# Attention and routed experts on one core: the last batch's end reordered, weight splits shared with GpSimd, rows without a token given addresses of their own

## The chip, the cores and the metric

The kernel runs on one core of one Trainium2 chip. The metric is the device time of one execution in microseconds (us), less is better; "the span" is the time from the first to the last instruction in the profiled execution. Engines: TensorE (PE in the rows, its weight loads PEld), VectorE (DVE), ScalarE (ACT), GpSimd (POOL) and SyncE (SP), which here only issues transfers. A "q" behind an engine's name is its sequencer, which issues transfers.

## The reference

`x` is 8 batches of 1024 tokens with 256 features, in f32.

```python
x = _layernorm(x + attention(x))           # 16 heads, latent 32, rotary, causal
# mixture of experts: E = 8, top K = 2, DIM = 256, H = 512
gates = softmax(xf @ gate_w); topw, topi = top_k(gates, 2)
topw = topw / sum(topw)
combine = sum(topw * one_hot(topi, 8))
h = gelu(ln(xf @ w1[e] + b1[e]) * ln1_g + ln1_b)   # for every expert e
y = h @ w2[e] + b2[e]
out = ln(sum(y * combine) + xf) * ln_g + ln_b
x = _layernorm(x + out)
```

## The kernel before

The program is a row of blocks; all engines meet at the end of each. In order:

1. `weight_phase`: the attention weights are combined. Here also the DRAM table `token_of_row` (67,584 rows of two integers: which token to read, which row of `y_rows` to write) is filled with "no token": read token 0, write row 2 * B * T, one row past the results. The fill is made by two memsets on VectorE into `no_token` and a transfer on SyncE's queue (line 88).
2. `attention_phase`, main block: 32 units (8 batches by 4 groups of 4 heads). Every engine walks one list of items in the order of `PLACES`, a table of places written out by hand. Items that belong to a batch's end are: `C` (TensorE multiplies the attention output by the projection, VectorE adds it to `z` and takes mean and variance, three instructions), `NORM` (GpSimd: 1/sqrt of the variance by a power), `NX` (VectorE normalizes), `ZT` (TensorE transposes, ScalarE copies to `z_T`), `G` (gate product, VectorE copies 8 logits), `STORE`, `R` (22 small VectorE steps of routing), `CNT` (counts on TensorE), `SCAT` (16 indirect transfers on GpSimd, line 805, which write token numbers into `token_of_row`). Items that use PSUM take turns in a ring of four banks.
3. The last batch's end is a block of its own (lines 864 to 947), because the expert weights take the place of the attention buffers. In it the 16 weight parts (`w1` and `w2` of 8 experts, 128x1024 each) are loaded by ScalarE's queue, and each is split in two: ScalarE makes the rounded high part (line 600), and a subtraction makes the low part in place (line 753, on VectorE); the text calls this subtraction a split. VectorE begins with a memset of the bias buffer, waits for five small tables, then makes splits 0 and 1, all `C` items, splits 2 to 5 between the `NX` items, `G`, `R`, the tables of tiles (lines 914 to 934), and then splits 6 to 15.
4. `expert_phase`: 136 tiles of 128 rows, sorted by expert. Per tile GpSimd gathers rows of `x1` (line 1007), makes a 1/sqrt (line 1013) and scatters the result to `y_rows` (line 1020); TensorE makes both products, each in three passes of high and low parts. ScalarE copies a tile's result out (line 1110). About 1,024 rows of these tiles hold no token. Each result scatter waits first for the landing of the one before it (lines 1018 and 1019).
5. `combine_phase`: 16 groups of 4 tiles are mixed, normalized and stored.

Of the kernel before, what the change touches and what calls it, by code (L numbers as in the profile page):

```python
# [6 lines left out]
F32, F32R, BF16 = mybir.dt.float32, mybir.dt.float32r, mybir.dt.bfloat16  # L7
# [5 lines left out]
P = 128  # L13
# [25 lines left out]
def weight_phase(nc, dram, wts, consts, lat_dram, token_of_row, xs):  # L39


    with ExitStack() as ctx:
# [27 lines left out]
        no_token = sb("no_token", [P, ROWS // P, 2], I32)  # L70
        zero_set = sem("zero_set")
# [8 lines left out]
        def _(sp):  # L80
# [6 lines left out]
            sp.wait_ge(zero_set, 2)  # L87
            sp.dma_start(token_of_row.rearrange("(p s) o -> p s o", p=P), no_token[:]).then_inc(tables_loaded, 16)
# [50 lines left out]
        def _(dve):  # L139
            nc.vector.memset(no_token[:, :, 0], 0).then_inc(zero_set, 1)  # L140
            nc.vector.memset(no_token[:, :, 1], 2 * B * T).then_inc(zero_set, 1)
# [51 lines left out]
def attention_phase(nc, dram, wts, consts, xs, lat_dram, inv_dram, x1_dram, token_of_row, routes, tail, attention,  # L193
# [9 lines left out]
    with ExitStack() as ctx:  # L203
# [66 lines left out]
        def unit_items(n):  # L270
# [36 lines left out]
            if g == GROUPS - 1:  # L307
                for name in ("C", "NX", "ZT", "G"):
                    put(name, *[(name, b, tb) for tb in range(TB)])
                put("NORM", ("NORM", b))  # L310
# [343 lines left out]
        def vector_items(dve, items):  # L654
            for it in items:
# [93 lines left out]
                elif kind == "W":  # L749
                    dve.wait_ge(w_hi_ready, n + 1)  # L750
# [22 lines left out]
        def gpsimd_items(pool, items, zero):  # L773
            for it in items:
# [21 lines left out]
                elif kind == "NORM":  # L796
# [3 lines left out]
                    nc.gpsimd.tensor_tensor(z_rstd[:], z_ve[:], half[:], ALU.pow).then_inc(rstd_ready, 1)  # L800
                elif kind == "SCAT":
# [7 lines left out]
        with nc.Block() as block:  # L809
# [20 lines left out]
            def _(pool):  # L830
# [21 lines left out]
        w_hi_ready, w_lo_ready = sem("e_hi_ready"), sem("e_lo_ready")  # L852
# [5 lines left out]
        scat_at, c_at = [it[0] for it in late].index("SCAT"), [it[0] for it in late].index("C")  # L858
        between = [x for it in late[c_at:scat_at] for x in
                   ((it, ("W", 2 + it[2] // 2)) if it[0] == "NX" and it[2] % 2 else (it,))]  # L860
        late = [("W", 0), ("W", 1)] + late[:c_at] + between + late[scat_at:]
        late_weights = [("W", w) for w in range(6, len(parts))]

        with nc.Block() as block:
# [22 lines left out]
            def _(act):  # L887
                for i, (w, e) in enumerate(parts):
                    act.dma_start(experts[w + "_lo"][:, e, :].bitcast(F32), dram[w][:, e, :]).then_inc(w_loaded[i], 16)
                scalar_items(act, late)  # L890
                scalar_items(act, late_weights)
# [4 lines left out]
            def _(dve):  # L896
                nc.vector.memset(experts["b2"][:].bitcast(F32), 0.0).then_inc(b_zeroed, 1)
                dve.wait_ge(end_tables, 16 * len(table_loads))
# [5 lines left out]
                vector_items(dve, late)  # L904
# [30 lines left out]
                vector_items(dve, late_weights)  # L935
# [559 lines left out]
```

## Time and profile before

| | us |
|---|---|
| runs of the kernel before | 2384.43, 2387.57, 2387.07 (median 2387.07) |
| profiled execution | 2383.96 |
| its span | 2382.2 |
| TensorE busy (share of the span) | 2119.7 (89%) |
| VectorE busy | 1715.5 (72%) |
| ScalarE busy | 1366.8 (57%) |
| GpSimd busy | 1296.8 (54%) |
| mean granted TensorE clock | 0.922 of full |

The profiled execution is one run; 1.8 us lie around its span. Busy shares are averages over blocks with different limits, so each block has to be read by itself: times below are counted from the span's start. A row of a timeline holds start, duration, engine, line and operation, how many instructions it merges (x5), and in brackets how long the engine stood idle before it and what released it. "issue" as a releaser is time in which the profile shows no wait.

### The profile page before, as it was taken

To read this page: it belongs to the slowest core of one execution; us is meant where nothing else is said; L and a number is where in the kernel's file an instruction comes from. 1 tells how busy PE (TensorE), PEld (TensorE's weight loads), DVE (VectorE), ACT (ScalarE), POOL (GpSimd) and SP (SyncE) were. 2 spreads that over 40 slices of the span, in tenths; PEclk is the share of its full clock that TensorE was granted. 3 is DMA by queue.
4 is the path that set the end of the run, shared out by engine and by line. 5 is a ranking of instruction groups with operands and counts; after the bars stand their busy time and mean duration, and the time that the engine had idled before them with its cause. 6 is when DMAs were issued, how large, how long until landed. Compare 5 with 4: busy or idle time off the path is not lost. (4 is left out here: it accounts for less than half of the span.)

```text
span 2382.2 us, 43666 instructions
## 1 busy us (share of the span) xinstructions
PE 2119.7 (89%) x12268; PEld 1476.8 (62%) x12268; DVE 1715.5 (72%) x5003; ACT 1366.8 (57%) x3316; POOL 1296.8 (54%) x1472
## 2 busy tenths in 40 slices
PE   3898998999899999899899989974399999999598
PEld 2654655565555556465566555533299989988487
DVE  3675687687577677668668767815588888888498
ACT  1265655555555565565565555653278778778254
POOL 2455465655754763666556475551677777776000
PEclk7798999999899898899899899985699999999799
DMA  6555556556555555554655555615022222222575
GB/s 181 123 137 129 113 114 160 116 113 156 116 118 147 121 122 123 133 121 108 163 111 126 143 119 115 135 24 199 23 75 75 75 73 75 75 73 66 165 245 169
DMA packets 190519, 284.47 MB, mean 119 GB/s; under 512 B 54072, under 2 KB 111056, under 8 KB 190160
## 3 DMA queue, kind: packets, MB, share of 16 engines
q1 hardware_dynamic: 168720, 236.43, 41.7%
q0 software_dynamic: 17152, 35.81, 5.0%
q10 hardware_dynamic: 4416, 9.44, 1.1%
q8 instruction: 110, 1.80, 0.3%
q14 instruction: 121, 0.99, 0.2%
HBM read 99.48 MB, written 37.90 MB: 58 GB/s over the span
## 5 line engine op out<-in xcount | busy, mean ns | idle before, releaser
L546 ACT ACTIVATE probs<-scores_T 128x512 f32<-128x512 f32 (+3 forms) x1536 | 654.7, 492 | 256.4 <-PE scores_T L435 253.0
L785 POOL TENSOR_SCALAR_AFFINE_SELECT probs<-probs 128x256 f32<-128x256 f32 x512 | 205.7, 410 | 540.1 <-ACT probs L546 537.4
L494 PE MATMUL ring<-k_stack,q_stack_b 96*128 96x512 f32 (+3 forms) x1024 | 400.7, 434 | 19.9 <-DVE neg_part L693 9.5
L693 DVE TENSOR_REDUCE neg_part<-ring 128x1 f32<-128x512 f32 x512 | 333.5, 684 | 97.5 <-PE ring L494 95.4
L435 PE MATMUL scores_T<-q_stack_b,k_stack 98*128 98x512 f32 (+3 forms) x1024 | 325.9, 396 | 43.8 <-ACT probs L546 42.7
L452 PE MATMUL o_ps<-probs,v_ones 128*17 128x512 f32 (+3 forms) x3072 | 349.6, 529 | 1.4 <-POOL probs L785 1.1
L494 PEld LDWEIGHTS ring<-k_stack,q_stack_b 96*128 96x128 f32 x1024 | 195.4, 200 | 228.4 <-issue 75.1
L698 DVE CUSTOM_DVE_ANT_0 ring<-ring,mask 128x384 f32<-128x384 f32 (+3 forms) x512 | 243.6, 507 | 120.4 <-PE ring L494 118.1
L698 DVE CUSTOM_DVE_ANT_0 ring<-ring,mask,neg_part 128x384 f32<-128x384 f32 (+3 forms) x512 | 260.5, 554 | 74.2 <-PE ring L494 73.4
L1099 ACT ACTIVATE o_sb<-ht_ps,ln_b,ln_g 128x128 f32<-128x128 f32 x544 | 217.9, 450 | 89.4 <-PE ht_ps L1048 89.0
L435 PEld LDWEIGHTS scores_T<-q_stack_b,k_stack 98*128 98x128 f32 x1024 | 192.0, 204 | 101.5 <-ACT probs L546 78.2
L554 ACT ACTIVATE u<-ring,lat_bias 128x512 f32<-128x512 f32 x128 | 88.0, 689 | 195.9 <-PE ring L476 184.3
L476 PE MATMUL ring<-x_hi,lat_w 128*128 128x512 f32 x512 | 189.8, 413 | 8.4 <-DMA lat_w<-lat_split 8.4
L494 PE MATMUL ring<-k_stack,q_stack_a 96*128 96x384 f32 (+3 forms) x512 | 171.8, 369 | 27.4 <-DMA k_stack<-u_rot 22.7
L762 POOL TENSOR_TENSOR u<-u,cos 128x512 f32<-128x512 f32 x126 | 162.1, 1287 | 36.6 <-DMA u_rot<-u 36.3
L1020 POOL DMA_INDIRECT y_rows<-z,tok x136 | 145.0, 1066 | 56.6 <-issue 33.7
L1007 POOL DMA_INDIRECT z<-x,tok x136 | 142.2, 1046 | 48.0 <-issue 40.0
L805 POOL DMA_INDIRECT token_of_row<-ids,slot x128 | 141.4, 1104 | 49.0 <-DVE ids_f L652 25.9
L770 POOL TENSOR_TENSOR u<-u,u_rot 128x512 f32<-128x512 f32 x126 | 162.4, 1289 | 9.2
L1060 PE MATMUL y_ps<-w_hi,g_hi 128*128 x544 | 165.1, 303 | 2.4 <-DVE g_lo L1126 1.7
L765 POOL TENSOR_TENSOR u_rot<-u_rot,sin 128x512 f32<-128x512 f32 x126 | 163.7, 1300 | 0.1
L494 PEld LDWEIGHTS ring<-k_stack,q_stack_a 96*128 96x128 f32 x512 | 93.6, 195 | 98.3 <-DVE neg_max L698 51.0
(191 smaller groups left out, 4617.1 us busy)
## 6 DMA issues: line engine op xcount, KB each, us to landing
u_rot<-u SPq DMA_DIRECT2D x128, 256.0 KB, 3.8
k_stack<-u_rot SPq DMA_DIRECT2D x128, 256.0 KB, 4.2
lat_w<-lat_split SPq DMA_DIRECT2D x32, 512.0 KB, 5.9
q_stack_a<-u_rot SPq DMA_DIRECT2D x64, 256.0 KB
q_stack_b<-u_rot SPq DMA_DIRECT2D x64, 256.0 KB
k_stack<-u SPq DMA_DIRECT2D x64, 256.0 KB, 4.3
y<-y_rows SPq DMA_DIRECT2D x32, 512.0 KB, 6.4
x_raw<-in_xT SPq DMA_DIRECT2D x16, 512.0 KB, 6.1
```

What stands on the lines that cost most here:

```text
L435: nc.tensor.matmul(sc[(t + j) % 3][:, HALF - w:HALF], k_stack[:, n % 2, h, P * kb:P * kb + P], q_stack[c][:, row_buf(n, c), h, q0 - HALF * ...
L452: last = nc.tensor.matmul(o_ps[32 * h:32 * h + VW, q0 - HALF * c:HALF], v_ones[:, b % 2, kb, HG * g + h, :], probs[:, s % 2, h, cols], sta ...
L476: last = nc.tensor.matmul(out[:], lat_w[:, kc, side, w_, :], a[:, kc, cols], start=i == 0, stop=i == 5)
L494: nc.tensor.matmul(out[:, 0:k1 - k0], q_stack[qb // 4][0:3 * L, row_buf(n, qb // 4), h, P * (qb % 4):P * (qb % 4) + P], k_stack[0:3 * L, n ...
L546: nc.scalar.activation(probs[:, s % 2, h, cols], sc[(t + j) % 3][:, HALF - w:HALF], ACT.Exp).then_inc(exp_done, 1)
L693: nc.vector.tensor_reduce(neg_part[:, n % 2, part_col], src[:], AX_X, ALU.max, negate=True).then_inc(max_taken, 1)
L698: nc.vector.tensor_tensor_reduce(out=src[:, 0:w], in0=src[:, 0:w], in1=consts["mask"][:, HALF - w:HALF], scale=-1.0, scalar=neg_part[:, n ...
L765: ops.tensor_tensor(u_rot[s][:, cols], u_rot[s][:, cols], consts["sin"][:, cols], ALU.mult).then_inc(sin_done[s], 1)
L770: ops.tensor_tensor(u[s][:, cols], u[s][:, cols], u_rot[s][:, cols], ALU.add).then_inc(rope_done[s], 1)
L785: nc.gpsimd.affine_select(both, both, [[0, 2], [1, P]], ALU.is_ge, zero, base=0, channel_multiplier=-1).then_inc(kept, 1)
L1060: nc.tensor.matmul(y_ps[j % 2][:, 0:C], a[j % 2][:, f, :], experts[w][:, bass.ds(e, 1), C * f:C * f + C], start=f == 0 and a is g_hi and w ...
L1099: nc.scalar.activation(g[k % 2][:, f, :], ht_ps[k % 2][:, P * f:P * f + P], ACT.Gelu, bias=experts["ln1_b"][:, f, bass.ds(e, 1)], scale=ex ...
```

## The change

Four edits.

- The table of empty rows comes from a kernel input `no_token` in DRAM, and row r of `token_of_row` without a token now writes row 2 * B * T + r of `y_rows`, which has grown by as many rows. The memsets and the wait for them are gone.
- A tile's result scatter no longer waits for the landing of the one before.
- In the last batch the transposes `ZT` stand one place earlier, so that the next tile's transpose comes ahead of this tile's gate product on TensorE. VectorE takes the `C` items ahead of the table wait.
- Splits 10 to 15 are made by GpSimd: 10, 11, 12 ahead of `NORM`, 13, 14, 15 between `NORM` and the scatters. VectorE makes splits 0 and 1 ahead of the first `G` and one behind each `G`. Weights are loaded and rounded in the order of `hi_order`: eight high parts ahead of the first `ZT` copy, one behind each.

```diff
-        no_token = sb("no_token", [P, ROWS // P, 2], I32)
-            sp.wait_ge(zero_set, 2)
-            sp.dma_start(token_of_row.rearrange("(p s) o -> p s o", p=P), no_token[:]).then_inc(tables_loaded, 16)
+            sp.dma_start(token_of_row.rearrange("(p s) o -> p s o", p=P), dram["no_token"]).then_inc(tables_loaded, 16)
-            nc.vector.memset(no_token[:, :, 0], 0).then_inc(zero_set, 1)
-            nc.vector.memset(no_token[:, :, 1], 2 * B * T).then_inc(zero_set, 1)
...
-                for name in ("C", "NX", "ZT", "G"):
+                for name in ("C", "NX", "G"):
                     put(name, *[(name, b, tb) for tb in range(TB)])
+                first, pace = PLACES["ZT"]
+                ahead = 1 if b == B - 1 else 0
+                at += [(first - ahead + pace * tb, ("ZT", b, tb)) for tb in range(TB)]
...
                 elif kind == "W":
-                    dve.wait_ge(w_hi_ready, n + 1)
+                    dve.wait_ge(w_hi_ready, hi_order.index(n) + 1)
...
+                elif kind == "W":
+                    pool.wait_ge(w_hi_ready, hi_order.index(n) + 1)
+                    w, e = parts[n]
+                    lo = experts[w + "_lo"][:, e, :]
+                    nc.gpsimd.tensor_tensor(lo, lo.bitcast(F32), experts[w + "_hi"][:, e, :].bitcast(F32),
+                                            ALU.subtract).then_inc(w_lo2_ready, 1)
...
-        scat_at, c_at = [it[0] for it in late].index("SCAT"), [it[0] for it in late].index("C")
-        between = [x for it in late[c_at:scat_at] for x in
-                   ((it, ("W", 2 + it[2] // 2)) if it[0] == "NX" and it[2] % 2 else (it,))]
-        late = [("W", 0), ("W", 1)] + late[:c_at] + between + late[scat_at:]
-        late_weights = [("W", w) for w in range(6, len(parts))]
+        weights = lambda a, b: [("W", w) for w in range(a, b)]
+        zt_at, c_end = late.index(("ZT", B - 1, 0)), late.index(("C", B - 1, TB - 1)) + 1
+        hi_order = (10, 0, 11, 1, 12, 2, 3, 13, 14, 4, 15, 5, 6, 7, 8, 9)
+        g_at = late.index(("G", B - 1, 0))
+        late_act = late[:zt_at] + [("W", w) for w in hi_order[:TB]] + [
+            x for it in late[zt_at:] for x in ((it, ("W", hi_order[TB + it[2]])) if it[0] == "ZT" else (it,))]
+        late_dve = late[c_end:g_at] + weights(0, 2) + [
+            x for it in late[g_at:] for x in ((it, ("W", 2 + it[2])) if it[0] == "G" else (it,))]
+        norm_at, scat_at = late.index(("NORM", B - 1)), late.index(("SCAT", B - 1, 0, 0))
+        late_pool = (late[:norm_at] + weights(10, 13) + late[norm_at:scat_at] + weights(13, len(parts)) + late[scat_at:])
...
             def _(dve):
                 nc.vector.memset(experts["b2"][:].bitcast(F32), 0.0).then_inc(b_zeroed, 1)
+                vector_items(dve, late[:c_end])
                 dve.wait_ge(end_tables, 16 * len(table_loads))
...
-                vector_items(dve, late)
+                vector_items(dve, late_dve)
...
-                vector_items(dve, late_weights)
                 dve.wait_ge(diff_exp, 1)
...
                     pool.wait_ge(y_ready, j + 1)
-                    if j:
-                        pool.wait_ge(y_stored[(j - 1) % 4], 16 * ((j - 1) // 4 + 1))
                     nc.gpsimd.indirect_dma_start(y_rows, bass.IndirectOffsetOnAxis(tok[:, j % 16, 1:2], 0),
...
-    y_rows = nc.dram_tensor("y_rows", (2 * B * T + 1, C), F32).ap()
+    y_rows = nc.dram_tensor("y_rows", (2 * B * T + ROWS, C), F32).ap()
+        "no_token": np.stack([np.zeros(ROWS), 2 * B * T + np.arange(ROWS)], 1).astype(np.int32).reshape(P, ROWS // P, 2),
```

## Rows read from the trace of the kernel before

**Rows 1.** Windows: length, busy us of PE, PEld, DVE, ACT, POOL; granted clock; DMA.

```profile
1609.00:1660.00 51.00, 24.39 (x89) 18.56 (x89) 25.80 (x74) 16.86 (x23) 4.58 (x4) 0.60 0.63 233
...
1800.00:1900.00 100.00, 100.00 (x697) 91.51 (x696) 86.98 (x221) 80.27 (x222) 78.04 (x85) 1.00 0.26 76
```

**Rows 2.** Timeline of ScalarE, last batch's end.

```profile
1609.38 10.06 ACTq L889 DMA_DIRECT2D w_lo<-in_w  x16
1619.48 4.84 ACT L600 ACTIVATE w_hi<-w_lo 128x1024 fp32r<-128x1024 f32 x5 [21.70 <-issue]
```

**Rows 3.** Timeline of VectorE, last batch's end.

```profile
1620.65 0.23 DVE L899 CAST ones<-rows 128x128 fp32r<-128x128 f32 x1 [9.02 <-DMA rows<-in_rows]
...
1623.72 0.41 DVE L717 TENSOR_TENSOR z<-ring,z 128x256 f32<-128x256 f32 x1
...
1631.52 0.18 DVE L721 BATCH_NORM_AGGREGATE z_mv<-z_stats 128x2 f32<-128x6 f32 x1
1633.84 0.73 DVE L726 TENSOR_SCALAR z<-z,z_mv,z_rstd 128x256 f32<-128x256 f32 x2 [2.13 <-POOL z_rstd L800]
1634.49 1.22 DVE L753 TENSOR_TENSOR w_lo<-w_lo,w_hi 128x1024 fp32r<-128x1024 f32 x1
...
1653.18 0.17 DVE L733 COPY logits<-ring 128x8 f32<-128x8 f32 x1 [1.91 <-PE ring L519]
...
1669.09 11.42 DVE L753 TENSOR_TENSOR w_lo<-w_lo,w_hi 128x1024 fp32r<-128x1024 f32 x10
```

**Rows 4.** Timeline of TensorE, last batch's end.

```profile
1611.95 6.31 PE L505 MATMUL ring<-cproj_w,y_T 128*128 128x256 f32 x16 [14.83 <-POOL y_T L791]
...
1643.83 0.99 PE L519 MATMUL ring<-gate_w,z_T 128*128 128x8 f32 x4 [0.57 <-ACT z_T L596]
```

**Rows 5.** Timeline of GpSimd, last batch's end.

```profile
1631.80 0.25 POOL L798 TENSOR_SCALAR z_ve<-z_mv 128x8 f32<-128x8 f32 x1 [19.99 <-DVE z_mv L721]
1632.13 1.67 POOL L800 TENSOR_TENSOR z_rstd<-z_ve,a_minus_half 128x8 f32<-128x8 f32 x1
1659.69 1.61 POOL L805 DMA_INDIRECT token_of_row<-ids,slot  x1 [25.89 <-DVE ids_f L652]
...
1669.10 12.28 POOL L805 DMA_INDIRECT token_of_row<-ids,slot  x1 [0.30 <-issue]
...
1691.78 0.96 POOL L805 DMA_INDIRECT token_of_row<-ids,slot  x1 [0.30 <-issue]
```

**Rows 6.** Line 791, all instructions: duration in ns, min/median/max.

```profile
L791 POOL TENSOR_TENSOR y_T<-y_T,inv_rep x16: 2346/2378/2822, 220.1 to 1609.5; 128x1024 f32<-128x1024 f32 x16
```

**Rows 7.** Line 684, all instructions, in the same form.

```profile
L684 DVE TENSOR_TENSOR u<-u,u_rot x64: 678/689/2785, 54.6 to 1521.5; 128x512 fp32r<-128x512 f32 x64
```

**Rows 8.** Timeline of VectorE near 415 us.

```profile
415.34 2.43 DVE L684 TENSOR_TENSOR u<-u,u_rot 128x512 fp32r<-128x512 f32 x1 [4.82 <-ACT u_rot L565]
```

**Rows 9.** Timeline of GpSimd near 415 us.

```profile
414.87 2.36 POOL L791 TENSOR_TENSOR y_T<-y_T,inv_rep 128x1024 f32<-128x1024 f32 x1 [0.22 <-DMA inv_rep<-inv_sums]
417.19 1.72 POOL L765 TENSOR_TENSOR u_rot<-u_rot,sin 128x512 f32<-128x512 f32 x1
```

**Rows 10.** Timeline of GpSimd, end of the expert block.

```profile
2199.37 1.30 POOL L1020 DMA_INDIRECT y_rows<-z,tok  x1 [0.20 <-issue]
2202.86 1.02 POOL L1020 DMA_INDIRECT y_rows<-z,tok  x1 [2.19 <-DMA y_rows<-z,tok]
...
2213.62 0.96 POOL L1020 DMA_INDIRECT y_rows<-z,tok  x1 [2.90 <-DMA y_rows<-z,tok]
```

**Rows 11.** Timeline of ScalarE, end of the expert block.

```profile
2205.61 0.38 ACT L1110 ACTIVATE z<-y_ps 128x256 f32<-128x256 f32 x1 [1.59 <-PE y_ps L1063]
```

**Rows 12.** Line 1020 in the window of its last scatter: issue to landing.

```profile
DMA to landing us min/median/max: 3.1/3.1/3.1
```

**Rows 13.** Line 1020, all 136 scatters.

```profile
DMA to landing us min/median/max: 2.5/2.5/4.2
```

**Rows 14.** DMA issues of the start: KB, us from issue to landing.

```profile
token_of_row<-no_token SPq DMA_DIRECT2D x1, 528.0 KB, 8.1
```

More of the change, by code:

```diff
@@ L69, in weight_phase @@
         vo_b_ready, lat_kept = sem("vo_b_ready"), sem("lat_kept")
-        no_token = sb("no_token", [P, ROWS // P, 2], I32)
-        zero_set = sem("zero_set")
         block = ctx.enter_context(nc.Block())
@@ L851, in attention_phase @@
         w_loaded = [sem(f"w_loaded{i}") for i in range(len(parts))]
-        w_hi_ready, w_lo_ready = sem("e_hi_ready"), sem("e_lo_ready")
+        w_hi_ready, w_lo_ready, w_lo2_ready = sem("e_hi_ready"), sem("e_lo_ready"), sem("e_lo2_ready")
         end_tables, b_loaded, ln1_loaded = sem("end_tables"), sem("b_loaded"), sem("ln1_loaded")
@@ L887, in _ @@
             def _(act):
-                for i, (w, e) in enumerate(parts):
+                for i in hi_order:
+                    w, e = parts[i]
                     act.dma_start(experts[w + "_lo"][:, e, :].bitcast(F32), dram[w][:, e, :]).then_inc(w_loaded[i], 16)
-                scalar_items(act, late)
-                scalar_items(act, late_weights)
+                scalar_items(act, late_act)
                 act.wait_ge(routed, R_STEPS * B)
@@ L940, in _ @@
                                         ALU.mult).then_inc(done, 1)
-                dve.wait_ge(w_lo_ready, len(parts))
+                dve.wait_ge(w_lo_ready, 10)
                 dve.wait_ge(done, 1)
@@ L945, in _ @@
             def _(pool):
-                gpsimd_items(pool, late, None)
+                gpsimd_items(pool, late_pool, None)
+                pool.wait_ge(w_lo2_ready, len(parts) - 10)
                 pool.wait_ge(scattered, 16 * 2 * TILES)
```

## Prediction

> **What bounds the kernel now.** I read the windows by stage first, then the timelines of the single engines between 1609 and 1700 us, then what each scatter waits for. The program is a row of blocks, and the change touches three: the weights at the start, the end of the last batch (1609.4 to 1696.6 us), and the expert tiles (1697 to 2222 us). In the expert block TensorE is busy 100.00 us of 100 at full granted clock [rows 1], so what another engine saves there is worth nothing until the last tiles. In the last batch's block TensorE works 24.39 us of 51 [rows 1], and the order is set by a chain across engines. Its stages before: ScalarE issues sixteen weight loads until 1619.4 and makes its first high part then [rows 2]; VectorE waits for a small table until 1620.65, makes two weight splits, and starts the first C item at 1623.72, though TensorE had begun them at 1611.95 [rows 3, 4]; the last variance is there at 1631.70 [rows 3]; GpSimd makes the inverse root by 1633.80 [rows 5]; VectorE normalizes, with four splits between, from 1633.84; the last gate logits come at 1653.35 and routing starts right behind them [rows 3]; then sixteen scatters run on GpSimd from 1659.69 to 1692.73 [rows 5]. One of these took 12.28 us where the last took 0.95, and it began at 1669.10, when VectorE began ten weight splits in a row (1669.09 to 1680.51) [rows 3, 5].
>
> **The change, part by part.** A split is an instruction on VectorE: 11.42 us for ten, 1.14 each [rows 3].
>
> C items. VectorE now takes them before the table wait. TensorE made the first four in 6.31 us [rows 4]; eight at that rate, begun at 1611.95, end at 1624.6. VectorE needs 1.0 us an item (1623.72 to 1631.70 for eight [rows 3]) and follows, so the variances are ready at 1625.6, 6.1 us earlier.
>
> Three splits on GpSimd (weights 10, 11, 12) now stand ahead of the root. The trace has no split on GpSimd. The nearest row is its product over the same 128x1024 elements: 2.35 us shortest, 2.38 median, 2.82 longest of 16 [rows 6]. I take 2.35, for its neighbours here are quiet, and keep 2.82 above; below, nothing suggests less. ScalarE's first high part ends at 1620.5 and each next one 0.95 later [rows 2]; the third one that GpSimd needs is the fifth, at 1624.3, so GpSimd is never short: 1620.5 + 3 x 2.35 = 1627.6. The root takes the 2.0 us from 1631.80 to 1633.80 [rows 5], so it ends at 1629.6 instead of 1633.8: 4.2 us gained, where without the three splits it would have been 6.1. The table casts, moved behind the C items, lie under this wait and cost nothing; uncovered they would be the 0.8 us from 1620.65 to the first split.
>
> What both engines read from SBUF. At 415.34 a VectorE subtraction of two SBUF tensors, 0.69 us at the median [rows 7], took 2.43 [rows 8]: it ended 0.5 us after GpSimd's product, 2.36 us long, ended at 417.23. GpSimd's next product in turn took 1.72 [rows 9], where half of a 2.35 us product is 1.2. The two are not run side by side: who comes second waits for the whole instruction. The Trainium skill says the same in "SBUF — State Buffer", section "Who interferes with whom": an exclusive lock, not a shared bandwidth; this trace agrees. So I let every GpSimd split after the root stand on VectorE's path. Split 13 has its high part (the eighth, 1627.2) and follows the root at once; it meets the first normalization: + 2.35, to 1632.0. Splits 14 and 15 meet VectorE's splits: + 4.7.
>
> Normalizing: eight, 0.65 us a pair (1633.84 to 1634.49) [rows 3], so 2.6, to 1634.6. Then ten splits, 11.4; eight logit copies of at most 0.17 [rows 3], mostly overlapped, 1.0; and the 4.7: routing starts at 1634.6 + 17.1 = 1651.7, 1.7 us earlier. Does TensorE keep up? Before, an iteration was 2.08 us (1.91 idle and 0.17 on VectorE [rows 3]), of which TensorE stood idle 0.57 ahead of the gate product [rows 4]; with the next transpose moved ahead of it this gap fills, and 8 x 1.5 = 12 us from 1632.4 ends at 1644.4, six us before VectorE. ScalarE needs a copy of 0.38 and a high part of 0.95, which also fits. The 8 x 0.57 = 4.6 us that the reordering frees on TensorE are thus worth nothing by themselves: VectorE is later.
>
> Routing to the first scatter is as before, 6.3 us: 1658.0. The scatters took 33.04 us. None of VectorE's splits is left beside them, so the long one becomes 0.96: 33.04 - 11.32 = 21.7. What the routing tables cost them stays (the first took 1.61 [rows 5]). End at 1679.7 instead of 1692.73: **13.0 us**. Bounds of this part: 7.05 more if GpSimd's last three splits run beside VectorE's work; 2.8 less if each of the six takes 2.82.
>
> Expert block. GpSimd loses one wait: a scatter had to wait until the scatter of the tile before had landed. Queued behind it on GpSimd are gathers and roots, for tiles far ahead; TensorE is full, so nothing in the steady part: 0. At the end it counts. The last five scatters started 3.5 to 3.9 us apart (2199.37, 2202.86, ..., 2213.62 [rows 10]), the last though its tile had been copied at 2205.99 [rows 11]. Without the wait: 1.0 us each plus 0.3 issue after 2200.67 gives 2201.0 and 2202.3; the next two wait for ScalarE alone, and the last starts at 2206.1. **7.5 us** gained. The last tiles hold rows without a token, all written to one address; the landing of the last took 3.1 us [rows 12] against a median of 2.5 for all [rows 13]. With rows of their own that is 0 to 0.6 more: I take 0.3.
>
> Start. Two memsets leave VectorE, which idled there until 10.9 us: 0. The table of empty rows comes from DRAM instead of SBUF: same place in SP's queue, same 528 KB, 8.1 us to landing before [rows 14], issued near 10.9, ended near 19.6 with the block ending at 26.2. No row shows a copy from DRAM to DRAM; below nothing, above I let its transfer double, 8 us more, which would end at 27.7 and cost 1.5, or up to 8 if what is queued behind moves with it whole. Bytes and queue stay, so I take 0.
>
> Sum: 13.0 + 7.5 + 0.3 = 20.8. The profiled execution took 2383.96 us (span 2382.2 and 1.8 around it), so its like would be 2363.2. It lay 3.1 below the median of the runs shown, 2387.07, and the same sum on that gives 2366.3; I forecast **2366**.
>
> **Rivals.** (a) *No lock between splits* (12%): GpSimd's last three run beside VectorE's, and 7.05 come on top: 2359. For it: the one long subtraction in [rows 8] could have had another cause. Against: its end, half a us behind GpSimd's.
>
> (b) *The long scatter stays* (8%). If it is not VectorE's splits that held it, but something in the scatter's own queue, 11.3 are not saved: 2378. Against: its start and end fit the ten splits within 0.9 us. The Trainium skill's "SBUF — State Buffer", same section, speaks against my reading: it infers that a two-input `tensor_tensor` takes only the read side and does not stall a GpSimd DMA's descriptors. By the rows it does, or a read of the offsets does; by that rule, this rival.
>
> (c) *Scatters land in turn anyway* (7%), or a second outstanding one waits in the queue: the 7.5 stay lost: 2374. Against: in the code the gaps are the semaphore wait that goes, and GpSimd stood idle 2.90 us ahead of the last one [rows 10].
>
> (d) *GpSimd's splits are dear* (6%), the other side. All six lie on the chain, three ahead of the root and three against VectorE. Each us more per split costs 6. At 2.35 + 20.8/6 = 5.8 us each the gain is gone; at 6.8 the result is 2393. Against: the same engine makes 1024 products in 2.35. A rounding output on GpSimd has no row.
>
> (e) *The copy at the start* (5%) moves the first block by up to 8: 2374.
>
> The rest, 62%, is my forecast, 2362 to 2370 by itself.
>
> **How the numbers follow.** The range leaves out (b) and (d), 14%, and takes in (a), (c), (e): 2357 to 2377. A measurement of this kernel tells about 0.2%, 4.8 us. Slower by more needs the dear half of (d) and what I have overlooked: 5%. No difference needs two rivals at once or the middle of (d): 4%. Faster: 91%.
>
> **What the profile would show.** First C item on VectorE near 1613.6; splits on GpSimd of about 2.4 us, with the root's end at 1629.6; a VectorE normalization or split of about 2.7 or 3.5 us beside each of the last three; routing near 1652; sixteen scatters in 22 us with none over about 2; expert tiles still 3.6 us apart; last four expert scatters 1.3 to 2.1 us apart, the last at ScalarE's last copy. Wrong would be: GpSimd splits of over 3.5 us, a long scatter with no split beside it, or a first block that ends after 26.7.

## The result and the profile after

| | median us | runs | lowest to highest |
|---|---|---|---|
| before | 2387.32 | 4 | 2384.43 to 2389.46 |
| changed | 2353.16 | 4 | 2338.54 to 2364.46 |

The ratio is 0.9862, 95% interval 0.982 to 0.9904: 34 us less, where 20.8 were forecast, and 4 us below the forecast's range. The profiled execution of the changed kernel is its fastest, 2338.54 us (span 2336.8, mean granted clock 0.939; before 2382.2 at 0.922). That difference in clock is the first thing to clear away. The ratios in this document leave out runs over 1.5% above the fastest of their kernel and are not the quotient of the two medians beside them (for p2_wait below the medians would give 0.992, its ratio is 0.9964).

The windows by stage, once for each kernel. The stages are cut at the same issues in both: the first `lat_w` load, the load of `b_raw` (start of the last batch's block), the first `tok` load (start of the expert tiles), the load of `ln_g_rep` (start of the combine stage). Columns as in [rows 1]. The changed kernel:

```profile
27.00:1589.20 1562.20, 1423.70 (x8079) 864.44 (x8079) 1101.78 (x3223) 875.14 (x1977) 887.45 (x1041) 0.94 0.55 125
1589.20:1663.10 73.90, 20.71 (x89) 17.12 (x89) 50.15 (x99) 18.13 (x25) 38.70 (x25) 0.57 0.43 161
1663.10:2177.15 514.05, 495.80 (x3400) 449.86 (x3400) 427.54 (x1088) 395.04 (x1089) 382.51 (x408) 0.98 0.25 72
2177.15:2336.80 159.65, 140.41 (x640) 122.98 (x640) 130.29 (x562) 77.19 (x225) 0.00 (x0) 0.94 0.68 213
```

The kernel before:

```profile
26.20:1609.40 1583.20, 1445.87 (x8079) 875.18 (x8079) 1094.57 (x3223) 876.02 (x1977) 887.56 (x1041) 0.92 0.54 123
1609.40:1697.60 88.20, 24.39 (x89) 18.56 (x89) 46.76 (x105) 18.46 (x25) 32.75 (x19) 0.56 0.37 135
1697.60:2222.20 524.60, 497.91 (x3400) 450.37 (x3400) 431.32 (x1088) 395.10 (x1089) 376.27 (x408) 0.97 0.24 70
2222.20:2382.20 160.00, 140.58 (x640) 123.09 (x640) 130.22 (x562) 77.23 (x225) 0.00 (x0) 0.94 0.68 212
```

The main block, 1583 us long, is the same code in both, with the same 8079 matmuls; TensorE needs 22.2 us less for them at a granted clock of 0.94 than at 0.92, and the block is 21.0 us shorter. Of the 45.4 us between the two spans, only 14.3 (last batch's block), 10.6 (expert tiles) and 0.4 (combine), less 0.8 at the start, lie in stages that the change can touch: 24.5 us. (Over all profiles of the two kernels, two and three, these stages differ by 26.5.) A second profile of the changed kernel (run t_after below), in a run at a mean clock of 0.928, gives the main block the length that it had before:

```profile
26.30:1609.30 1583.00, 1445.66 (x8079) 876.88 (x8079) 1100.98 (x3223) 876.01 (x1977) 888.49 (x1041) 0.92 0.54 123
```

Now the last batch's block. VectorE, in the view of [rows 3]:

```profile
1593.96 0.42 DVE L715 TENSOR_TENSOR z<-ring,z 128x256 f32<-128x256 f32 x1 [2.41 <-PE ring L503]
...
1602.51 0.18 DVE L719 BATCH_NORM_AGGREGATE z_mv<-z_stats 128x2 f32<-128x6 f32 x1
1602.61 0.52 DVE L909 CAST ones<-rows 128x128 fp32r<-128x128 f32 x1
1603.05 2.45 DVE L911 CAST b_hi<-b_raw 8x256 fp32r<-8x256 f32 x1
1605.53 2.46 DVE L913 TENSOR_TENSOR b_lo<-b_raw,b_hi 8x256 fp32r<-8x256 f32 x1
1609.89 4.70 DVE L724 TENSOR_SCALAR z<-z,z_mv,z_rstd 128x256 f32<-128x256 f32 x8 [1.90 <-POOL z_rstd L798]
1614.51 2.35 DVE L751 TENSOR_TENSOR w_lo<-w_lo,w_hi 128x1024 fp32r<-128x1024 f32 x2
...
1616.85 3.30 DVE L751 TENSOR_TENSOR w_lo<-w_lo,w_hi 128x1024 fp32r<-128x1024 f32 x1
...
1620.15 3.29 DVE L751 TENSOR_TENSOR w_lo<-w_lo,w_hi 128x1024 fp32r<-128x1024 f32 x1
...
1623.44 1.21 DVE L751 TENSOR_TENSOR w_lo<-w_lo,w_hi 128x1024 fp32r<-128x1024 f32 x1
...
1630.62 0.21 DVE L609 TENSOR_REDUCE top<-logits 128x8 f32<-128x64 f32 x1
```

GpSimd, in the view of [rows 5]:

```profile
1600.68 7.03 POOL L803 TENSOR_TENSOR w_lo<-w_lo,w_hi 128x1024 fp32r<-128x1024 f32 x3 [8.95 <-ACT w_hi L598]
...
1608.19 1.67 POOL L798 TENSOR_TENSOR z_rstd<-z_ve,a_minus_half 128x8 f32<-128x8 f32 x1
1609.84 2.33 POOL L803 TENSOR_TENSOR w_lo<-w_lo,w_hi 128x1024 fp32r<-128x1024 f32 x1
1614.58 7.78 POOL L803 TENSOR_TENSOR w_lo<-w_lo,w_hi 128x1024 fp32r<-128x1024 f32 x2 [2.40 <-ACT w_hi L598]
1636.77 1.61 POOL L809 DMA_INDIRECT token_of_row<-ids,slot  x1 [14.41 <-DVE ids_f L650]
...
1639.96 2.02 POOL L809 DMA_INDIRECT token_of_row<-ids,slot  x1 [0.30 <-issue]
...
1657.55 0.95 POOL L809 DMA_INDIRECT token_of_row<-ids,slot  x1 [0.30 <-issue]
```

TensorE, in the view of [rows 4], the eight C items:

```profile
1591.88 8.96 PE L503 MATMUL ring<-cproj_w,y_T 128*128 128x256 f32 x32 [14.83 <-POOL y_T L789]
```

In microseconds from the start of the block (1609.4 before, 1589.2 after):

| | before | forecast | after |
|---|---|---|---|
| last variance there | 22.3 | 16.2 | 13.5 |
| inverse root ends | 24.4 | 20.2 | 20.7 |
| eight normalizations end | between splits | 25.2 | 25.4 |
| routing starts | 44.0 | 42.3 | 41.4 |
| first of the sixteen scatters | 50.3 | 48.6 | 47.6 |
| last of them ends | 83.3 | 70.3 | 69.3 |
| block ends | 88.2 | | 73.9 |

A small cast and a small subtraction (8x256 elements) took 2.45 and 2.46 us: they stood behind the GpSimd splits that began at 1600.68. GpSimd's last two splits lost time too: they took 7.78 us together, where one alone takes 2.33. The scatters took 21.73 us (1636.77 to 1658.50); none was over 2.02.

The end of the expert tiles. GpSimd, in the view of [rows 10]:

```profile
2162.55 1.30 POOL L1028 DMA_INDIRECT y_rows<-z,tok  x1 [0.20 <-issue]
2164.15 0.96 POOL L1028 DMA_INDIRECT y_rows<-z,tok  x1 [0.30 <-issue]
2165.41 0.96 POOL L1028 DMA_INDIRECT y_rows<-z,tok  x1 [0.30 <-issue]
2167.47 0.96 POOL L1028 DMA_INDIRECT y_rows<-z,tok  x1 [1.09 <-ACT z L1118]
2169.30 0.96 POOL L1028 DMA_INDIRECT y_rows<-z,tok  x1 [0.88 <-ACT z L1118]
```

ScalarE's last copy, in the view of [rows 11]; then line 1028 in the window of its last two scatters, as [rows 12]; then the copy at the start, as [rows 14]:

```profile
2168.64 0.38 ACT L1118 ACTIVATE z<-y_ps 128x256 f32<-128x256 f32 x1 [1.45 <-PE y_ps L1071]
```

```profile
DMA to landing us min/median/max: 2.4/2.5/2.5
```

```profile
token_of_row<-in_no_token SPq DMA_DIRECT2D x1, 528.0 KB, 7.0
```

From ScalarE's last copy (its end) to the end of the stage it was 2222.2 − 2205.99 = 16.2 us and is 2177.15 − 2169.02 = 8.1. But the stage is 10.6 shorter, not 8.1: the last copy itself comes 2.5 us earlier in it (505.5 us after its start, 508.0 before). The forecast had 0 there.

### The profile page after: what moved, and what is told of

It reads as the page before. It is cut to its first block and busy times, and to the rows that moved or that the text cites. A ratio compares the mean times of both kernels' runs of the same rounds, so it can differ in the third digit from the quotient of the medians.

```text
span 2336.8 us, 43530 instructions
## 1 busy us (share of the span) xinstructions
PE 2092.7 (90%) x12268; PEld 1464.7 (63%) x12268; DVE 1721.4 (74%) x4995; ACT 1365.5 (58%) x3316; POOL 1308.8 (56%) x1478
## 5 line engine op out<-in xcount | busy, mean ns | idle before, releaser
L492 PE MATMUL ring<-k_stack,q_stack_b 96*128 96x512 f32 (+3 forms) x1024 | 396.3, 429 | 22.1 <-DVE neg_part L691 10.4
L433 PE MATMUL scores_T<-q_stack_b,k_stack 98*128 98x512 f32 (+3 forms) x1024 | 318.1, 387 | 45.4 <-ACT probs L544 44.5
L450 PE MATMUL o_ps<-probs,v_ones 128*17 128x512 f32 (+3 forms) x3072 | 341.8, 518 | 2.1 <-POOL probs L783 1.8
L433 PEld LDWEIGHTS scores_T<-q_stack_b,k_stack 98*128 98x128 f32 x1024 | 186.3, 198 | 99.6 <-ACT probs L544 78.6
L492 PE MATMUL ring<-k_stack,q_stack_a 96*128 96x384 f32 (+3 forms) x512 | 170.9, 367 | 25.5 <-DMA k_stack<-u_rot 20.8
L1017 POOL DMA_INDIRECT z<-x,tok x136 | 147.5, 1084 | 47.8 <-issue 40.4
L1068 PE MATMUL y_ps<-w_hi,g_lo 128*128 x544 | 154.2, 283 | 0.0
L1068 PE MATMUL y_ps<-w_lo,g_hi 128*128 x544 | 153.8, 283 | 0.0
```

Of the source, the lines that this page charges most:

```text
L433: nc.tensor.matmul(sc[(t + j) % 3][:, HALF - w:HALF], k_stack[:, n % 2, h, P * kb:P * kb + P], q_stack[c][:, row_buf(n, c), h, q0 - HALF * ...
L450: last = nc.tensor.matmul(o_ps[32 * h:32 * h + VW, q0 - HALF * c:HALF], v_ones[:, b % 2, kb, HG * g + h, :], probs[:, s % 2, h, cols], sta ...
L492: nc.tensor.matmul(out[:, 0:k1 - k0], q_stack[qb // 4][0:3 * L, row_buf(n, qb // 4), h, P * (qb % 4):P * (qb % 4) + P], k_stack[0:3 * L, n ...
L1068: nc.tensor.matmul(y_ps[j % 2][:, 0:C], a[j % 2][:, f, :], experts[w][:, bass.ds(e, 1), C * f:C * f + C], start=f == 0 and a is g_hi and w ...
```

## The experiments

Twelve more entries ran in three groups, repeats among them, each group beside the kernel before on one chip. In each group the kernel before ran 17 to 35 times, and that gave the first surprise: 2362.73 to 2414.33 us, 2357.32 to 2400.63 and 2373.97 to 2401.81, where the three runs shown ahead of the forecast lay within 3.2 us.

**One part alone: s1_start and s2_late.** The first has only the start edit; the second is the changed kernel with the start and the dropped wait undone.

```diff
# s1_start, against the kernel before
-            sp.wait_ge(zero_set, 2)
-            sp.dma_start(token_of_row.rearrange("(p s) o -> p s o", p=P), no_token[:]).then_inc(tables_loaded, 16)
+            sp.dma_start(token_of_row.rearrange("(p s) o -> p s o", p=P), dram["no_token"]).then_inc(tables_loaded, 16)
-            nc.vector.memset(no_token[:, :, 0], 0).then_inc(zero_set, 1)
-            nc.vector.memset(no_token[:, :, 1], 2 * B * T).then_inc(zero_set, 1)
-    y_rows = nc.dram_tensor("y_rows", (2 * B * T + 1, C), F32).ap()
+    y_rows = nc.dram_tensor("y_rows", (2 * B * T + ROWS, C), F32).ap()
# s2_late, against the changed kernel: the lines above turned round, and
+                    if j:
+                        pool.wait_ge(y_stored[(j - 1) % 4], 16 * ((j - 1) // 4 + 1))
```

> The kernel before with the first edit alone: the table of empty rows comes from DRAM, rows without a token have addresses of their own; the scatter's wait and the last batch's end are as before. After the change the main attention block took 20.9 us less in the profiled run although its code is the same, and the first block ended 0.85 us later. Theory S (this edit moves the start of the main block, and that alone changes which stretches of it get the lower granted clock): the main block gets about 10 to 20 us shorter, ratio 0.992 to 0.996. Theory N (this edit does nothing; the main block varies by itself from run to run in every kernel): 0.85 us longer, ratio 1.000 within the spread. My prediction's sum: within 1 us of before.

> The kernel before with the last batch's end alone: reordered, six splits on GpSimd; the start and the scatter's wait are as before. Theory S: the main block is as before (about 1583 us in the profile), the last batch's block 14.4 us shorter, ratio 0.994. Theory C (what comes later in the program, its size or its placement, changes the main block): the main block some 10 us shorter as well, ratio 0.990.

**The start of the main block moved: s3_later3 and s4_later6.** Three or six more additions of 128x256 on VectorE ahead of the last weight of the first block; their result is not used.

```diff
# s3_later3, against the kernel before; s4_later6 has 6
+            for i in range(3):
+                nc.vector.tensor_tensor(pause[:, i, :], m_ps[:, 0:C], cproj_b[:], ALU.add)
             nc.vector.tensor_tensor(wts["z_bias"][:], m_ps[:, 0:C], cproj_b[:], ALU.add).then_inc(split, 1)
```

> The kernel before with three more VectorE additions of 0.3 to 0.4 us (into a buffer that nobody reads) at the end of the first block, so that the main block starts about 1.0 us later. No part of the change is in it. Theory S (start of the main block against the clock): the main block gets shorter by 10 us or more, or at least its length moves by more than 3 us. Theory N: 1 us slower, ratio 1.0004.

> As the kernel with three additions, with six: the main block starts about 2.0 us later. Theory S: the main block's length moves again, in either direction, and differs from that with three additions. Theory N: 2 us slower, ratio 1.0008.

Measured in this group (before 2390.43, 35 runs): s1_start 2383.32 us, ratio 0.9966 (0.9931 to 1.0001); s2_late 2375.95, 0.9945 (0.9912 to 0.9978); s3_later3 2390.84, 1.003 (0.9998 to 1.0062); s4_later6 2386.99, 1.0005 (0.9977 to 1.0033). 12 runs each. The lengths of the stages, with all later profiles, all cut at the same issues:

| profile | start | main | last batch | expert | combine | mean clock |
|---|---|---|---|---|---|---|
| before | 26.2 | 1583.2 | 88.2 | 524.6 | 160.0 | 0.922 |
| t_before | 26.7 | 1582.6 | 87.8 | 527.7 | 159.4 | 0.922 |
| s1_start | 27.3 | 1594.2 | 87.6 | 524.9 | 160.5 | 0.919 |
| s3_later3 | 27.9 | 1574.7 | 87.3 | 529.3 | 160.6 | 0.928 |
| s4_later6 | 27.9 | 1562.6 | 87.3 | 525.9 | 161.4 | 0.932 |
| s2_late | 26.8 | 1583.6 | 73.6 | 525.8 | 160.1 | 0.927 |
| p2_wait | 25.9 | 1580.6 | 73.6 | 523.0 | 159.1 | 0.925 |
| t_startwait | 26.6 | 1576.1 | 87.4 | 514.9 | 158.8 | 0.930 |
| changed | 27.0 | 1562.3 | 73.8 | 514.1 | 159.7 | 0.939 |
| q_after | 26.0 | 1575.1 | 73.9 | 514.2 | 159.3 | 0.931 |
| t_after | 26.3 | 1583.0 | 73.6 | 514.7 | 159.1 | 0.928 |
| p3_vector | 26.5 | 1584.0 | 70.6 | 514.2 | 160.4 | 0.925 |
| p4_psum | 26.9 | 1593.9 | 63.2 | 514.6 | 158.9 | 0.923 |
| t_psum | 26.3 | 1572.4 | 61.7 | 515.3 | 159.6 | 0.936 |

The columns that a kernel's edit touches repeat to within 1.5 us in most pairs of like kernels (the expert stage with the wait within 6.3); the main block, which no edit touches, goes from 1562 to 1594 and follows the clock, not the kernel: s4_later6, otherwise the kernel before, has the same 1562 as the changed kernel. Starting that block 1 to 2 us later brings nothing that the times show. The late edit alone has 14.6 us in its stage (73.6 against 88.2), its main block is as before, and its ratio is the 0.994 of its stages. s1_start shows nothing in its stages; its interval reaches 1.0001, and its profile has the longest main block of all.

**The changed kernel again, and with the wait put back: q_after and p2_wait.** p2_wait is the changed kernel with the two lines of the wait of s2_late.

> The changed kernel again, to time it against more runs of the kernel before. In the first comparison it was 1.4% faster on four runs, 34 us; the profiled run had a main block of 1562 us, and five other kernels with the same main block had 1563 to 1594. Theory N (the main block varies by itself, and four runs happened on short ones): over more runs the change gives what the stages show, 14.4 in the last batch's block, 10.5 in the expert block, less 0.85 at the start, so 24 us, ratio 0.990. Theory C (the change shortens the main block): ratio 0.986 or below again, and a main block near 1562 us again. My prediction: 20.8 us, ratio 0.991.

> The changed kernel with the scatter's wait for the landing before it put back; rows without a token still have addresses of their own. Prediction's theory: the expert block 7.5 to 8 us longer than in the changed kernel, all of it behind ScalarE's last copy; the tiles before that as in the changed kernel. Rival (the wait also cost TensorE time in the steady part, for the changed kernel's expert block was 2.5 us shorter up to the last copy than before's): 10.5 us longer, 2.5 of them ahead of the last copy. Rival (the same address for all empty rows cost the 2.5): 8 us longer only.

The times of both stand below, with their group. p2_wait's expert stage is 8.7 us longer than the mean of the changed kernel's three (523.0 against 514.3): 2.6 ahead of ScalarE's last copy and 6.1 behind it. So the forecast's theory, all of it behind the last copy, fails; the rival that puts 2.5 ahead of it has that part right. The addresses don't explain that part: with the wait the last copy starts 508.4 and 509.6 us into the stage in the two kernels with addresses of their own (p2_wait, s1_start), 508.0 to 511.3 in the five with one address. But the addresses do count behind the last copy. The last scatters of p2_wait:

```profile
2192.14 0.96 POOL L1030 DMA_INDIRECT y_rows<-z,tok  x1 [2.19 <-DMA y_rows<-z,tok]
2195.28 0.96 POOL L1030 DMA_INDIRECT y_rows<-z,tok  x1 [2.17 <-DMA y_rows<-z,tok]
```

They start 3.14 us apart, where with one address it was 3.85 (2209.77 to 2213.62 [rows 10]). From the start of the last copy to the end of the stage it is 16.6 to 18.1 us with one address and the wait, 14.6 and 15.3 with addresses of their own and the wait, and 8.5 without the wait.

**The splits off GpSimd: p3_vector and p4_psum.** In p3_vector VectorE makes all sixteen: ten where the changed kernel has them, the six of GpSimd behind the routing, beside the scatters. p4_psum does the same with seven, but ScalarE first copies the raw half to PSUM, and VectorE subtracts from there, so only one operand of each is in SBUF. It differs from p3_vector in the order too: the high parts come in plain order again, split 0 stands ahead of the normalizations, and one split fewer stands ahead of routing.

```diff
# p3_vector, against the changed kernel
-        late_pool = (late[:norm_at] + weights(10, 13) + late[norm_at:scat_at] + weights(13, len(parts)) + late[scat_at:])
+        late_pool = late
                 nc.vector.tensor_copy(routes["expert"][:], expert_f[0:1, :])
+                vector_items(dve, weights(10, len(parts)))
# p4_psum, against p3_vector
-                vector_items(dve, weights(10, len(parts)))
+                vector_items(dve, [("WP", w) for w in range(9, len(parts))])
# WP on ScalarE, and on VectorE
+                    nc.scalar.activation(raw_ps[n % 2][:], experts[w + "_lo"][:, e, :].bitcast(F32),
+                                         ACT.Identity).then_inc(w_copied, 1)
+                    nc.vector.tensor_tensor(experts[w + "_lo"][:, e, :], raw_ps[n % 2][:],
+                                            experts[w + "_hi"][:, e, :].bitcast(F32), ALU.subtract).then_inc(w_lo_ready, 1)
```

> The changed kernel with all sixteen splits on VectorE: 10 to 15 behind the tables of tiles, beside the scatters, none on GpSimd. Theory L (SBUF lock between the two engines, as in the prediction): the root ends 5 us earlier against the block's start (three GpSimd splits and two casts go from its front), the normalizations take 2.6 us instead of 4.7 and the splits of VectorE 1.2 us each with none of 3.3, so routing starts 11 us earlier; and one scatter is held for the six splits, about 7.8 us instead of 0.96. The last batch's block is then 4 to 5 us shorter than in the changed kernel. Rival (descriptors are not held by a two-input subtraction; the long scatter before came from elsewhere): no scatter over 2.1 us, the block 11 us shorter.

> As the kernel with all splits on VectorE, but the seven last splits (9 to 15), beside the scatters, read the raw weight from PSUM, where ScalarE, idle by then, has put a copy; only one of their inputs is then in SBUF. Split 0 stands ahead of the normalizations, split 1 behind them, 2 to 8 behind the gate copies. Theory L: a subtraction with one SBUF input doesn't hold the scatters, none takes over about 2.1 us, and the last batch's block is 61 to 63 us, 11 to 13 less than in the changed kernel. Rival (any stream of VectorE work on SBUF, its writes too, holds GpSimd's descriptors): one scatter of about 9 us, the block about 70 us.

Measured (before 2390.01, 17 runs): q_after 2353.47 us, ratio 0.9863 (0.9822 to 0.9905), 6 runs; p2_wait 2371.39, 0.9964 (0.9923 to 1.0004), 12 runs; p3_vector 2357.46, 0.9856 (0.9807 to 0.9905), 6 runs; p4_psum 2344.04, 0.9794 (0.9755 to 0.9833), 6 runs. The changed kernel repeats its 0.986, which is theory C's ratio, but its interval reaches theory N's 0.990 and its main block is not near 1562 (1575.1). p2_wait's interval reaches 1.0004, while its stages would give 0.992. p3_vector's time is not told apart from q_after's.

The six splits beside the scatters, in p3_vector: VectorE, then GpSimd.

```profile
1626.90 2.67 DVE L724 TENSOR_SCALAR z<-z,z_mv,z_rstd 128x256 f32<-128x256 f32 x8 [1.57 <-POOL z_rstd L798]
...
1656.98 6.88 DVE L751 TENSOR_TENSOR w_lo<-w_lo,w_hi 128x1024 fp32r<-128x1024 f32 x6
```

```profile
1657.00 7.74 POOL L809 DMA_INDIRECT token_of_row<-ids,slot  x1 [0.30 <-issue]
1665.04 0.96 POOL L809 DMA_INDIRECT token_of_row<-ids,slot  x1 [0.31 <-issue]
```

And the seven in t_psum, the same kernel as p4_psum (in p4_psum's own profile too no scatter is over 2.03 us):

```profile
1643.48 8.37 DVE L757 TENSOR_TENSOR w_lo<-raw_ps,w_hi 128x1024 fp32r<-128x1024 f32 x7
```

```profile
1643.49 0.96 POOL L821 DMA_INDIRECT token_of_row<-ids,slot  x1 [0.30 <-issue]
...
1654.85 0.96 POOL L821 DMA_INDIRECT token_of_row<-ids,slot  x1 [0.30 <-issue]
```

The long scatter begins with the splits and lasts as long as they do: ten splits, 12.28 us [rows 5]; six, 7.74; none, no long one. With seven that read one operand from PSUM, 8.37 us of them, the scatters beside them stay at 0.96. So the subtraction holds an indirect DMA's issue on GpSimd when both its operands are in SBUF, and not when one is in PSUM. The shorter delay fits too: the third scatter, 2.02 or 2.03 us long before, in the changed kernel, in p3_vector and in t_psum, begins beside a 1.29 us comparison of two SBUF operands (1639.85 and the scatter at 1639.96 in the changed kernel). The Trainium skill's "SBUF — State Buffer", section "Who interferes with whom", has the rule for the PSUM form (a VectorE instruction with at most one SBUF input, outside the modes that use both of its port pairs, does not contend with GpSimd), and the trace agrees. Its inference that `tensor_tensor` leaves descriptor generation alone is what the 7.74 us speak against, if descriptors are what is held; it could also be the read of the offsets, and no run here tells the two apart. One SBUF tensor as input is by itself no safeguard: the normalizations and the small cast of the changed kernel have one and were held by GpSimd's splits.

p3_vector also prices the sharing with GpSimd. Without it the eight normalizations take 2.67 us, not 4.70, the two splits of 3.30 and 3.29 are 1.21, and the root does not wait for three splits: routing starts 31.0 us into the block, 10.4 earlier than in the changed kernel. The long scatter gives 6.8 of that back. The block is 3.3 us shorter than that of the changed kernel: sharing costs more than the long scatter that it avoids. That is read from the stage; the runs' medians, 2357.46 and 2353.47, don't show it. Against p3_vector the block of p4_psum and t_psum is 7.4 and 8.9 us shorter; 6.8 of this is the long scatter, the rest goes with the other order.

**The noise of the comparison, the wait alone, and repeats: t_before, t_startwait, t_after, t_psum.** t_before and t_after are the two kernels unchanged, t_psum is p4_psum again, t_startwait is s1_start with the wait dropped:

```diff
# t_startwait, against s1_start
                     pool.wait_ge(y_ready, j + 1)
-                    if j:
-                        pool.wait_ge(y_stored[(j - 1) % 4], 16 * ((j - 1) // 4 + 1))
```

> The kernel before, unchanged, entered as if it were a change: what the comparison itself gives for nothing. Both theories: a ratio whose interval holds 1, a span whose stages are those of the kernel before (late block 88, expert stage 525, combine stage 160 us), and a main block anywhere from 1563 to 1594 us, by how much of it is granted the lower clock.

> The start edit and the dropped wait, without the late edit. By the stages: late block 87 to 88 us, expert stage 514 to 516 (the kernel with the wait has 523 to 526), everything else as before, so 8 to 10 us below the kernel before, ratio 0.996 to 0.9965. If dropping the wait is what shortens the main block as well (theory M, a real gain of some 10 us there), ratio 0.992 or less and a mean clock over the runs above that of the kernel before by 0.005 or more.

> The changed kernel once more, beside the other three. Theory N (the main block has no systematic gain; its medians were low by chance of the granted clock): ratio near the stages' 24.5 us, 0.9897, interval reaching it. Theory M (the main block is granted more of the higher clock in the changed kernel): 0.9863 again, 0.9845 to 0.988, with a mean granted clock 0.005 or more above that of the kernel before.

> The version in which no split lies on GpSimd and VectorE reads the raw half of the late splits from PSUM, once more. Late block 63 us, expert stage 514.5. Its stages are 35 us shorter than those of the kernel before in sum: ratio 0.985 by theory N, 0.979 again by theory M.

Measured (before 2383.84, 23 runs): t_before 2389.43 us, ratio 1.0024 (0.9994 to 1.0055), 12 runs; t_startwait 2375.6, 0.9961 (0.993 to 0.9993), 12 runs; t_after 2358.44, 0.9897 (0.9858 to 0.9937), 6 runs; t_psum 2346.71, 0.9833 (0.9795 to 0.9871), 6 runs. Two medians of one kernel in one group differ by 5.6 us, more than the 4.8 that the prediction took for what a measurement can tell. And the changed kernel comes out at 0.9897, the value of its stages (24.5 of 2384 us). Theory M asked for a mean granted clock 0.005 or more above the kernel before: t_after has 0.926 and t_startwait 0.924 over their runs, the kernel before 0.924. In this group theory N holds for both. t_psum, with 0.9305, lies between the two theories (0.9833, where they gave 0.985 and 0.979).

The steady part of the expert tiles. GpSimd's groups by line over the 420 us from 42 us after the stage's start, first before, then changed; the last column is the engine's idle time ahead of the group and what ended it:

```profile
L1020 POOL DMA_INDIRECT y_rows<-z,tok x116 | 123.9, 1068 | 42.2 <-issue 29.2 <-DMA y_rows<-z,tok 6.0 <-ACT z L1110 3.6
L1007 POOL DMA_INDIRECT z<-x,tok x116 | 121.8, 1050 | 35.3 <-issue 35.3
L1013 POOL TENSOR_TENSOR h_rstd<-h_ve,minus_half 128x1 f32<-128x1 f32 x116 | 75.9, 654 | 21.5 <-DVE h_ve L1158 19.6 <-DMA y_rows<-z,tok 0.5
```

```profile
L1017 POOL DMA_INDIRECT z<-x,tok x117 | 127.7, 1092 | 35.7 <-issue 35.7
L1028 POOL DMA_INDIRECT y_rows<-z,tok x116 | 122.6, 1057 | 24.5 <-issue 24.5
L1023 POOL TENSOR_TENSOR h_rstd<-h_ve,minus_half 128x1 f32<-128x1 f32 x117 | 78.9, 674 | 31.3 <-DVE h_ve L1166 30.9
```

The idle time ahead of GpSimd's scatters is 17.7 us less without the wait, that ahead of its roots 9.8 more.

And TensorE is not quite full with the wait. Windows of 100 us, of the kernel before (150 us into the stage), of t_before (200) and of the changed kernel (200):

```profile
1847.00:1947.00 100.00, 99.48 (x688) 90.25 (x687) 86.13 (x219) 79.13 (x219) 75.80 (x83) 1.00 0.26 74
```

```profile
1897.05:1997.05 100.00, 98.84 (x670) 88.10 (x669) 84.49 (x213) 77.11 (x213) 71.51 (x80) 1.00 0.25 72
```

```profile
1863.10:1963.10 100.00, 100.00 (x697) 91.53 (x696) 86.98 (x222) 80.15 (x222) 78.13 (x84) 1.00 0.26 76
```

The busy share says less than the number of matmuls: with 98.84 us busy there are 670, with 100.00 there are 697, and a tile has 25. In the seven profiles with the wait ScalarE's last copy starts 508.0 to 511.3 us into the stage (mean 509.5); in the seven without it 505.5 to 506.8 (mean 506.0), whichever of the other edits the kernel has. The steady part is worth 3.5 us.

More than half of it is lost in two places that are the same in all seven profiles with the wait. GpSimd, before, ahead of the 53rd of the 136 scatters, and the root behind it; then what VectorE does with this root:

```profile
1915.31 1.06 POOL L1020 DMA_INDIRECT y_rows<-z,tok  x1 [3.21 <-ACT z L1110]
1916.67 0.96 POOL L1007 DMA_INDIRECT z<-x,tok  x1 [0.30 <-issue]
1917.65 0.58 POOL L1013 TENSOR_TENSOR h_rstd<-h_ve,minus_half 128x1 f32<-128x1 f32 x1
```

```profile
1918.27 0.55 DVE L1147 TENSOR_SCALAR h_norm<-h_norm,h_mv,h_rstd 128x512 f32<-128x512 f32 x1 [1.62 <-POOL h_rstd L1013]
```

The same scatter in the changed kernel:

```profile
1878.99 1.06 POOL L1028 DMA_INDIRECT y_rows<-z,tok  x1 [1.04 <-issue]
```

GpSimd works its queue in order, so the scatter that is held (3.21 us, 2.9 to 3.4 in the seven) holds the root of a later tile; VectorE's normalization waits for the root, TensorE for the normalization, and ScalarE's 58th copy comes 4.72 us behind the 57th instead of 3.60. It repeats at the 106th scatter (held 2.62) and the 111th copy (4.55). Together these cost 2.0 to 2.4 us; without the wait the two scatters are held 1.04 us, and no copy there is late. The rest is smaller delays in places that differ from run to run. The scatter before the held one took 3.2 us to land, in the changed kernel too. But it had landed by 1911.9, and what holds GpSimd from there to 1915.31 is not shown: the copy that the row names is one of a later tile, and this tile's had ended at 1907.6.

## Why the prediction was wrong, point by point

The forecast was 2366 us, range 2357 to 2377, faster at 0.91. The sign and most of the mechanisms held; the time fell below the range.

- *Routing and scatters, 13.0 us.* Right, measured 14.3 in the stage. The scatters are 21.73 us against 21.7 forecast. The C items were ready 8.8 us earlier instead of 6.1 (32 matmuls in 8.96 us where eight at the rate of the first four had given 12.6), which was worth nothing, since GpSimd's three splits, not the variances, set the root.
- *The lock, 7.05 us.* Right in kind, a little too dear: splits that met lost 2.09 us each and the normalizations 2.03 (4.70 against 2.67), 6.2 in sum. This 0.85 and the routing's own 6.15 us (6.3 forecast) are the 1.0 us by which the first scatter came earlier than forecast; that the root came 0.5 later is made up by the other splits and logit copies, 0.5 shorter. Rival (a) falls: a VectorE split is 3.30 us beside one on GpSimd and 1.21 without.
- *The long scatter.* Right; rival (b) falls, by p3_vector and t_psum.
- *Splits on GpSimd at 2.35 us.* Right: 2.33 alone. Rival (d) falls. But their price is what they hold up, and in this block it is higher than what they save.
- *Last scatters and landing, 7.5 + 0.3.* The sum is right, 8.1 from the last copy on; the split is not. By p2_wait and s1_start the dropped wait is worth 6.1 to 6.8 us of it and the addresses 1.3 to 2.0, not 0.3: before, each of the last scatters waited for a landing that was slow, and the forecast counted only the last landing (3.1, now 2.5). Rival (c) falls: the scatters start 1.26 to 2.06 us apart.
- *Start, 0.* Right: 25.9 to 27.3 us in the nine profiles with the edit, 26.2 to 26.8 in the three that have neither the edit nor added pauses. Rival (e) falls: the copy from DRAM landed in 7.0 us, not 8.1.
- *"TensorE is full, so nothing in the steady part: 0."* This is the step that failed. [rows 1] show 100.00 us busy of 100 in one window; others of the same stage, not read, have 99.48, and 98.84 in t_before. What the forecast left out is that GpSimd works in order: a scatter that waits holds up roots that TensorE needs. The 3.5 us are the largest missing term of a stage: with it and 14.3 and 8.1 the sum is 25.9, the forecast would have been 2361, and a range moved by as much would hold 2353.16.
- *The time from which the sum is taken.* The other failure. Three runs within 3.2 us of each other, and 4.8 us as what a measurement can tell, stood for a kernel whose 91 runs in all go from 2357.32 to 2414.33, median 2387.9. The 16 runs of the changed kernel have a median of 2356.3, which is 31.6 less; the first four, at 2353.16, lay low, one of them at the highest clock seen. The three ratios are 0.9862, 0.9863 and 0.9897, where the stages give 0.989 to 0.990. The third group's 2358.44 us is inside the forecast's range; that the first four runs fell below it is in part chance.

What stays open is the rest, 31.6 less 25.9, some 6 us. Part is the spread: t_before shows 5.6 us between two samples of one kernel. The mean granted clock over the 16 runs is 0.928, over the runs of the kernel before 0.923; 0.003 of this is the shorter last batch's block alone (see below), and the other 0.002 is about 4 us at 17 us for each 0.01, an estimate. Whether the changed kernel also tends to a slightly shorter main block, these runs don't settle; its own profiles have 1562.3, 1575.1 and 1583.0 there, those of the kernel before 1583.2 and 1582.6.

The fastest version is p4_psum: 0.9794 and 0.9833 in its two groups, 9 us and 12 below the changed kernel beside it. It keeps the `C` items first, the earlier transposes, the dropped wait and the start, and takes the splits off GpSimd.

## What to carry to other kernels

A busy share of 100% in one window does not make a stage full: read several, count the matmuls, and ask what stands in order behind the wait, before it is priced at nothing. GpSimd is no free helper for VectorE where both read SBUF: each overlap is paid almost in full by who comes second (2.03 to 2.18 us of a 2.33 us split), and putting one operand in PSUM through an idle ScalarE freed the scatters. Cut the span into stages at issues that both kernels share, and compare those, when a code that is unchanged can differ by more than the effect looked for.

## What the runs showed of the hardware

- The time of one kernel on one core follows the granted clock of TensorE. Of the kernel before, in one group, a run at a mean of 0.939 took 2357.32 us and one at 0.915 took 2397.61: 40 us for the same instructions, 17 us for each 0.01.
- In the last batch's block the granted clock is 0.56 to 0.57 of full, that is mostly the lower level, 1.2 GHz, with TensorE busy 24.4 us of 88.2 and 20.7 of 73.9. Cutting this block therefore raises the mean clock without any gain in the other stages: 0.44 x 88.2 less 0.43 x 73.9 is 7.0 us, or 0.003 of the mean, an estimate.
- VectorE's small instructions are held too, a cast and a subtraction of 8x256 elements: 0.27 and 0.41 us in p3_vector, 2.45 and 2.46 beside GpSimd's splits.
- Indirect scatters that each wait for the landing of the one before start 3.14 us apart when rows without a token have addresses of their own, and 3.70 to 3.85 when these rows share one address (p2_wait; before [rows 10]).
- An indirect scatter's issue on GpSimd takes 0.96 us, 7.74 with six two-operand SBUF subtractions beside it on VectorE, and 0.96 with seven that read one operand from PSUM.
